# A graph-attention edge stage: counting every 16th key, a weight-stationary second expert layer, eight row buffers

## The reference

```
x = relu(sum over 32 paths of bn-conv(1x1, 3x3, 1x1)(x) + x)      # convolution
t = t + local attention(layernorm(t))                              # 7x7 window, 8 heads
t = t + mixture of experts(layernorm(t))                           # gates from a graph attention
```

```
h = x_flat @ W_gat                      # [M, 4 heads, 4 experts]
e = leaky_relu(a_src[src] + a_dst[dst]) # one value per edge and head
alpha = softmax of e over the edges of one dst
agg = segment_sum(h[src] * alpha, dst)  # then layernorm, mean over heads: scores
w = softmax of the two best scores
out += g[e] * (gelu(x @ W1[e] + b1[e]) @ W2[e] + b2[e])   # for 4 experts, 64 -> 128 -> 64
```

## Time and profile before

| | us |
|---|---|
| runs, median of 3 (lowest, highest) | 5598.91 (5587.48, 5601.15) |
| profiled execution, first to last instruction | 6624.5 |
| of it TensorE busy | 3002.6 (45%) |
| VectorE busy | 3002.1 (45%) |
| GpSimd busy | 2970.5 (45%) |
| ScalarE busy | 1456.9 (22%) |

### The profile page before, as it was taken

How to read it: one execution, slowest core, us unless ns; L and a number is a source line. 1 busy time by engine, 2 the same in 40 slices (tenths; PEclk the granted TensorE clock), 3 DMA queues, 4 the chain that set the end, 5 groups by cost and what they waited for, 6 DMA issues and landing times. The chain is left out here.

```text
span 6624.5 us, 60648 instructions
## 1 busy us (share of the span) xinstructions
PE 3002.6 (45%) x16592; PEld 2109.7 (32%) x16592; DVE 3002.1 (45%) x4301; ACT 1456.9 (22%) x5679; POOL 2970.5 (45%) x3274
## 2 busy tenths in 40 slices
PE   2888888869999760000444241311313130130620
PEld 1445455458888650000233120200202120120410
DVE  5888888649999731010899120110101011010358
ACT  0334343348888510000000010000000000010110
POOL 1000000026667537777000657575675757667045
PEclk9788888769999855555555555555555555555555
DMA  6566556646666450000000011110111111011143
GB/s 141 87 95 96 94 94 95 95 75 102 101 104 103 87 146 8 8 7 8 3 3 3 10 37 25 34 28 14 45 15 34 25 34 28 14 45 15 58 166 118
DMA packets 583690, 381.06 MB, mean 58 GB/s; under 512 B 404996, under 2 KB 524852, under 8 KB 577748
## 3 DMA queue, kind: packets, MB, share of 16 engines
q1 hardware_dynamic: 384376, 216.58, 14.6%
q10 hardware_dynamic: 89403, 109.89, 9.4%
q0 software_dynamic: 109728, 52.69, 6.7%
HBM read 232.80 MB, written 145.29 MB: 57 GB/s over the span
## 5 line engine op out<-in xcount | busy, mean ns | idle before, releaser
L1569 POOL DMA_INDIRECT e_row<-scratch_table,e_edge x2048 | 2014.2, 983 | 989.2 <-issue 680.8
L1750 PE MATMUL f_psY<-f_w,f_hid 128*128 128x64 f32 x1568 | 363.0, 425 | 1657.4 <-ACT f_hid L1701 1292.2
L1633 DVE TENSOR_TENSOR f_y<-f_psY,f_b 128x1024 f32<-128x1024 f32 x49 | 59.8, 1219 | 2298.5 <-DMA scratch_t<-t 1711.2
L1750 PEld LDWEIGHTS f_psY<-f_w,f_hid 128*128 128x128 f32 x1568 | 342.5, 330 | 1753.4 <-ACT f_hid L1701 1371.8
L1608 DVE TENSOR_TENSOR i_hot<-f_psH,i_digit 128x1024 bf16<-128x1024 f32 x512 | 582.3, 1211 | 640.0 <-DMA scratch_parts<-h2p 356.8
L1701 ACT ACTIVATE f_hid<-f_psH,f_b 128x512 f32<-128x512 f32 x196 | 131.4, 687 | 2933.9 <-PE f_psH L1745 1351.7
L1733 PE MATMUL f_psH<-i_hot 128*128 128x128 bf16 x2048 | 264.8, 310 | 958.3 <-DVE i_hot L1608 761.2
L964 POOL MEMSET a_wproj<- 128x128 f32 x1 | 0.2, 210 | 1367.4 <-POOLq L161 1367.4
L1077 ACT ACTIVATE prob<-psS,low 128x100 f32<-128x100 f32 x1568 | 514.1, 373 | 61.9 <-DVE low L1110 61.9
L1733 PEld LDWEIGHTS f_psH<-i_hot 128*128 128x128 bf16 x2048 | 197.3, 140 | 1025.7 <-DVE i_hot L1608 825.7
L472 PE MATMUL psH<-h,c_w 128*128 128x448 f32 x1008 | 511.5, 595 | 3.8 <-ACT h L584 2.0
(11 more groups left out here) (281 smaller groups left out, 5329.9 us busy)
## 6 DMA issues: line engine op xcount, KB each, us to landing
stack<-scratch_parts ACTq DMA_DIRECT2D x504, 112.0 KB
e_row<-scratch_table,e_edge POOLq DMA_INDIRECT x2048
scratch_y<-f_y ACTq DMA_DIRECT2D x49, 512.0 KB
scratch_state<-e_state SPq DMA_DIRECT2D x16, 1536.0 KB, 6.0
g_y<-scratch_y SPq DMA_DIRECT2D x24, 1024.0 KB
val<-scratch_vpad SPq DMA_DIRECT2D x672, 35.0 KB
scratch_parts<-h2p ACTq DMA_DIRECT2D x56, 336.0 KB, 3.3
keys<-scratch_kpad SPq DMA_DIRECT2D x112, 155.0 KB
```

The costliest lines, as they stand in the source:

```text
L1569: pool.indirect_dma_start(out=row[s][:, f, :], out_offset=None, in_=table_dram, in_offset=bass.IndirectOffsetOnAxis(ap=edge[s][:, 0, f:f + ...
L1750: m = pe.matmul(psY[par][:, j, e * C:(e + 1) * C], hid[e][:, j * 128:(j + 1) * 128], w2[:, e, :], start=True, stop=True)
```

## The change

It changes five things together.

First, the count. `Index` stores digits only for the last key of each group of 16 (`digit` is [128, 2, 128], `GROUP` = 16). The one-hots and matmuls count these: 16 groups instead of 256. The running sum gives, for each node, the one group of 16 keys in which its run ends (`group_ix`, semaphore `grouped`).

Second, GpSimd gathers these groups, 128 indirect DMAs of 64-byte rows of the sorted keys, one per column of nodes; VectorE counts how many of the 16 keys are at most the node's number, and so has the exact end of each run; its begin is the end of the node before, for a row's first node fetched from the partition above with a small DMA. Then the positions are `placed` as before.

Third, GpSimd's order: key groups, row gathers of chunk 0, first node's a_dst and the 128 scatters, row gathers of chunks 1 to 15. The small store after the scatters goes to SP.

Fourth, `AHEAD` = 8 row and edge buffers. To have the room, the one-hot tiles lie in the last row buffer, the zeros in `e0` and the keys in `part`. All loops of the phase are written out, with constant waits.

Fifth, the experts' second layer holds the weights still: `w2` is padded so that two experts share one 128-channel output, 4 matmuls of 512 columns a tile; the result has channels on partitions (`scratch_y` is [256, tokens]). ScalarE adds the bias while it copies from PSUM. Where ScalarE's exponentials of the chunks stand among the tiles is a list, `EXPS_AFTER`. `finish_phase` loads y by channel and turns it on TensorE, 16 transposes a chunk, into PSUM, from where VectorE scales it; TensorE's first turn stands before the transposes of the carries.

```diff
-AHEAD = 4
+AHEAD = 8
+KEYS_BEFORE, RUNS_BEFORE = 0, 1
+EXPS_AFTER = (14, 15, 16, 17, 18, 22, 25, 29, 33, 36, 40, 44, 47, 49, 49, 49)
...
+        group = part_i[:, 0:EF // GROUP]
+        lasts = dst[:].rearrange("p (g k) -> p g k", k=GROUP)[:, :, GROUP - 1]
...
-                for s in range(AHEAD):
-                    gather(0, s)
-                pool.wait_ge(const_in, 48)
-                pool.indirect_dma_start(out=b_first[:], out_offset=None, in_=adst_dram,
...
+                def group_keys():
+                    pool.wait_ge(grouped, 1)
+                    for t in range(128):
+                        pool.indirect_dma_start(out=keys[:, t, :], out_offset=None, in_=key_rows,
+                                                in_offset=bass.IndirectOffsetOnAxis(ap=group_ix[:, t:t + 1], axis=0)).then_inc(keys_in, 16)
...
+                for c in range(NFC):
+                    if c == KEYS_BEFORE:
+                        group_keys()
+                    if c == RUNS_BEFORE:
+                        first_of_run()
+                    gather(c)
...
-                with dve.Fori(0, NFC // 2) as turn:
-                    for par in range(2):
-                        dve.wait_ge(digit_in[par], (turn + 1) * 16)
-                        for g in range(GROUPS):
+                for g in range(GROUPS):
+                    dve.wait_ge(hot_used, g)
...
+                done(dve.tensor_scalar(inc[:], inc[:], float(GROUPS_ALL - 1), None, ALU.min))
+                dve.tensor_copy(group_ix[:], inc[:]).then_inc(grouped, 1)
...
+                dve.wait_ge(keys_in, 16 * 128)
+                done(dve.tensor_scalar(keys, keys, SRC_BITS, NODES - 1, ALU.logical_shift_right, ALU.bitwise_and))
+                done(dve.tensor_copy(keyf, keys))
+                dve.wait_ge(const_in, 48)
+                done(dve.tensor_tensor(keyf, keyf, node_id[:].unsqueeze(2).to_broadcast([128, 128, GROUP]), ALU.is_le))
+                done(dve.tensor_reduce(inside[:], keyf, AX.X, ALU.add))
+                dve.scalar_tensor_tensor(upto[:], inc[:], float(GROUP), inside[:], ALU.mult, ALU.add).then_inc(summed_up, 1)
...
+                for c in range(NFC):
+                    sp.wait_ge(scanned, c + 2)
+                    sp.dma_start(state_view[c], state[c % 2][:]).then_inc(state_out[c % 2], 16)
+                    if c + AHEAD < NFC:
+                        sp.dma_start(edge[c % AHEAD][:], edge_dram[c + AHEAD]).then_inc(edge_in[c % AHEAD], 16)
...
-                        for j in range(ZT // 128):
-                            m = pe.matmul(psY[par][:, j, e * C:(e + 1) * C], hid[e][:, j * 128:(j + 1) * 128], w2[:, e, :],
-                                          start=True, stop=True)
+                        m = pe.matmul(psY[par][:, e // 2, :], w2[:, e, :], hid[e][:], start=e % 2 == 0, stop=e % 2 == 1)
...
+                def turn(k):
+                    s, (lo, hi) = k % SLOTS, CHUNKS_AT[k]
+                    pe.wait_ge(y_in[s], loads(k))
+                    wait(pe, scale_done, k - 1)
+                    for j in range(hi - lo):
+                        for a in range(2):
+                            m = pe.transpose(psM[k % 2][:, j, 2 * a:2 * a + 2, :].rearrange("p e c -> p (e c)"),
+                                             y[s][:, a, j * 128:(j + 1) * 128], ident[:])
+                    m.then_inc(y_turned, 1)
```

More of the change, by code:

```diff
@@ L1227, in step @@
             dve.wait_ge(self.done, 5)
-            dve.tensor_copy(out[:, :, 5, :], chunks(part_i)).then_inc(self.digits, 1)
+            dve.tensor_copy(self.digit[:, 1, :], group).then_inc(self.digits, 1)
         elif i == 7:
@@ L1464, in edge_phase @@
         b_first = sb("e_b_first", [128, GHEADS])
[L1465 to L1468, removed]
+        iota = sb("i_iota", [128, 128]); before = sb("i_before", [128, 128]); node_id = sb("i_node_id", [128, 128])
+        digit = sb("i_digit", [128, 2, FC])
         zero = sb("i_zero", [128, 128], BF16)
@@ L1480, in edge_phase @@
         part = sb("e_part", [128, FC, GH])
-        w1 = sb("f_w1", [C, EXPERTS, 128]); b1 = sb("f_b1", [128, EXPERTS]); w2 = sb("f_w2", [128, EXPERTS, C])
-        b2 = sb("f_b2", [128, EXPERTS * C])
+        zeros = e0
+        keys = part[:].bitcast(I32)
+        keyf = state[0][:, :, 0:GROUP]
+        spare = row[AHEAD - 1][:].rearrange("p f c -> p (f c)").bitcast(BF16)
+        hot = [[spare[:, (2 * i + d) * HOT * 128:(2 * i + d + 1) * HOT * 128].rearrange("p (c x) -> p c x", x=128) for d in range(2)] for i in range(2)]
@@ L1527, in _ @@
                 for c in range(NFC):
[L1528 to L1532, removed]
+                    sp.dma_start(flat[c], zeros[:].rearrange("p f h -> p (f h)")).then_inc(b_zeroed, 16)
@@ L1587, in _ @@
-                with pool.Fori(1, NFC // AHEAD) as turn:
-                    for s in range(AHEAD):
-                        gather(turn, s)
+                def group_keys():
[3 more added lines that the diff above has]
+                                                in_offset=bass.IndirectOffsetOnAxis(ap=group_ix[:, t:t + 1], axis=0)).then_inc(keys_in, 16)
@@ L1711, in both @@
-                def both(turn, last):
-                    for par in range(2):
-                        for q in range(par * PER, (par + 1) * PER):
-                            gelus(turn, q, not last or q < 2 * PER - 1)
-                        exps(turn, par)
-                with act.Fori(0, NFC // 2 - 1) as turn:
-                    both(turn, False)
-                both(NFC // 2 - 1, True)
-                gelus(NFC // 2, 0, False)
-                act.wait_ge(y_out[0], 16 * (TILES_Z // 2 + 1))
@@ L1724, in _ @@
+                for par in range(2):
+                    act.wait_ge(y_out[par], 16 * ((TILES_Z + 1 - par) // 2))
             @block.tensor
@@ L1814, in finish_phase @@
         of_slot = lambda k: range(k % SLOTS, k + 1, SLOTS)
-        loads = lambda k: 16 * sum(1 + spans_of(*CHUNKS_AT[i]) for i in of_slot(k))
+        loads = lambda k: 16 * len(of_slot(k))
         stores = lambda k: 16 * sum(spans_of(*CHUNKS_AT[i]) for i in of_slot(k))
@@ L2049, in _ @@
                 m.then_inc(turned, 1)
+                turn(0)
                 pe.wait_ge(carried, 1)
@@ L2053, in _ @@
                 m.then_inc(turned_back, 1)
+                pe.wait_ge(fix_limited, 1)
+                for k in range(1, NCH):
+                    turn(k)
             @block.scalar
@@ L2130, in build_program @@
         table_phase(nc, io, range(N), t2, z, table, adst, index=index)
-    edge_phase(nc, io, z, table, adst, digit, edge, node, first, b, state, y)
-    finish_phase(nc, io, state, node, first, ends, table, adst, y, t2, out)
+    with ExitStack() as lasting:
+        edge_phase(nc, lasting, io, ordered, z, table, adst, digit, edge, node, first, b, state, y)
+        finish_phase(nc, lasting, io, state, node, first, ends, table, adst, y, t2, out)
 def kernel(**inputs):
```

287 lines of the change are left out of this document (147 added, 140 removed).

## The result

The changed kernel takes 5777.45 us (median of 4 runs, 5769.58 to 5781.56) against 5600.03 us before: ratio 1.0312, 95% interval 1.0294 to 1.0329, slower by 177 us. The forecast was 5756 us, from 5590 to 5850.

The account below looks back on a forecast made before the run. GpSimd's chain of gathers was taken to set the end of the edge stage. The terms summed to +157.4 us on 5661, giving 5819; less the 62 us offset, 5756 us, range 5590 to 5850.

Parts of the forecast that it names:

- the 1025 us: Profiled span 6624.5 us against 5598.9 timed; read as recording delaying TensorE's completions, absent from timed runs; removing delays gives 5661.
- start wait: Before the first gather: GpSimd waits for the short count, first gather at 2494.8 instead of 2448.2, +46.6 us (44 to 60).
- tables: Table stage: the smaller digit store holds SP's next issue for less time, -5 us (0 to -11).
- key gathers: Edge stage: 128 more indirect DMAs on GpSimd at 1.304 us each, +166.9 us (160 to 179).
- chunk 0's wait: After the scatters: with eight row buffers GpSimd no longer waits for chunk 0's scan, -40.1 us.
- 2048 row gathers: Edge stage: the first 512, at 1.352 us, might go at 1.304; between -24 and nothing, -12 us taken.
- tail: After the last gathers: the last chunk's b scan is now ahead of its rows, -2 us.
- finish: Last phase: chunk 0's turn on TensorE stands ahead of the carry transposes and sums gathers wait, +3 us (0 to +10).
- offset of -62 us: The timed 5599 lies 62 us below the 5661 left after removing delays from the trace; carried over to the forecast.
- third rival: Slower still: 1.352 us spacing is what gathers beside an undisturbed TensorE cost, for all of them; 5854 us, chance 6%.
- Waits real: First rival: TensorE's completions come late in timed runs too, so GpSimd's idle time is real; faster, 4918 us, chance 13%.
- the second: Second rival: a share of the wait is real, the count ending some 150 us after 512 gathers; 5600 us, chance 5%.

Follow-up runs that it names:

- before_again: The kernel before, unchanged, profiled and timed once more: ratio 0.9997 to the kernel before, profiled span 5618.5 us.
- late_keys: The changed kernel with key groups gathered after chunk 0's rows and scatters after chunk 1's: 5733.57 us, ratio 1.0224 to the kernel before.
- full_count_eight: The changed kernel with the count of all keys put back, no key groups, scatters behind chunk 3: 5568.86 us, ratio 0.9926 to the kernel before.
- one_key_gather: The changed kernel with one of the 128 key gathers instead of all: 5620.41 us, ratio 1.0006 to the kernel before.
- before_eight_buffers: The kernel before with eight row and edge buffers, scatters still behind chunks 0 to 3: 5587.66 us, ratio 0.9956 to the kernel before.
- before_short_count: The kernel before counting only every 16th key, without key groups: 5605.15 us against 5610.79, ratio 0.9993.
- weights_in_psum: full_count_eight with the edge weights written to PSUM and one output buffer for the experts: 5533.30 us, ratio 0.9833 to the kernel before.

## Why the prediction was right, point by point

Direction and size hold, and so does the mechanism of the change: GpSimd's chain of indirect DMAs sets the end, the full count was hidden, the key groups and the start wait are new on the chain. The cause that the prediction gave for the 1025 us was wrong, and the sum came out closer than its terms. The terms, from the start of one step to the start of the next in the profiles of before_again (5618.5 us) and of the kernel after (5774.2):

| step | predicted, us | in the profiles, us | timed alone |
|---|---|---|---|
| start wait | +46.6 | +43.0 (2446.12 in late_keys to 2489.11) | 49 (late_keys) |
| tables | -5 | -4.6 (full_count_eight 2450.67, late_keys 2446.12; same chip) | |
| key gathers | +166.9 | +162.7 | 171 (one_key_gather) |
| chunk 0's wait | -40.1 | -31.9 (33.2 between last scatter and next gather; 1.3) | -25 (before_eight_buffers) |
| 2048 row gathers | -12 | +0.7 (2655.6; 2656.3) | |
| tail | -2 | -1.2 (28.3; 27.1) | |
| finish | +3 | -9.2 (279.4; 270.2) | |
| sum | +157.4 | +155.7 by the spans | +177 |

(The rows add up to 159.5. Of the 3.8 us between, 3.6 come from the first gather: it starts at 2454.24 us in before_again and at 2450.67 in full_count_eight, on another chip.)

**Luck in the sum.** The forecast was 12.7 us too low for the row gathers and 8.2 too low for chunk 0's wait, and 12.2 too high for the finish, 4.2 for the key gathers and 3.6 for the start. They cancel to 2 us. That the sum fits so well is luck; that the two large terms fit within 5 us is not.

**Start, keys, tables.** Right within 5 us each. (A third of the 11.20 us of the earlier trace rows would be 3.7 for the tables, not the 5 that was taken.) The spacing of the key gathers was 1.272 us, between the 1.25 and the 1.304 of the prediction, since no scan stands beside them.

**The reading of the 1025 us.** Right that the timed kernel does not have them, by the sum, and this carried the sign of the forecast. Wrong in its cause: "the cost of recording". Two consequences of that cause, stated in the prediction, failed. In the changed kernel late completions were to let TensorE do only three or four tiles in 167 us; the 248 matmul records in the 163 us of key gathers are 15 tiles and a half. And recording would have to hit every profile, while before_again shows none of it. The sign that the prediction had set for this reading (a span near 5820 us and a timed run within 1.5% of it) came true all the same: it fits any cause that is missing from timed runs, and could not tell recording from one disturbed execution. That a wrong cause led to the right conclusion rests on the sum alone, which took the delays out whatever they were. Why TensorE's completions came late in that execution stays open.

**The offset of -62 us.** It was carried as if it lay in the scale of the trace. It did not: before_again spans 5618.5 us where the sum gave 5661, and 39.8 of these 42.5 us are the first stretch (692.1 us for 512 gathers; 652.3 from 2454.24 to 3106.54 here), 8.2 chunk 0's wait (41.4 against 33.2, from the last scatter's start to the next gather's), less 6.0 by which the stage starts later. So the high spacing of that stretch, 1.352, was the disturbance as well: in it GpSimd idled for 0.86 us every 22.4 us, once for each pair of one-hot tiles, and 27 of the 512 gathers took over 1.1 us; in before_again there is neither. This decides the third rival: 2048 row gathers take the same in both kernels, and 1.352 never returns. The 12 us taken off for it was a step to leave out.

**Chunk 0's wait.** Mis-sized: 33.2 us undisturbed, of which 30.2 show as a wait, so that 31.9 go where the forecast took 40.1 from the disturbed trace. The timed saving of the buffers alone, 25 us (0.28 to 0.60%), agrees with that within its interval.

**The finish.** Wrong in sign. The turn before the carries costs what was said (carries are turned at 5522.38, 2.6 us after they were ready), but the sums gathers, which bound this phase, get shorter by 164.0 - 143.5 = 20.5 us, because the scaling pass no longer holds them. Only 9.2 us of it reach the end: 2.2 us go to the later start of these gathers, and behind the last of them the phase takes 61.5 us where it took 52.3. Part of that is VectorE's, which now waits longer for its chunks (21.8 us in total before its scaling passes in full_count_eight, 14.3 in before_eight_buffers); the rest no run attributes. The prediction weighed what the transposes cost TensorE and not what VectorE's operand in PSUM does to GpSimd.

**What is left.** The profiles give +155.7, the timed medians +177. The kernel before has a median of 5619.6 us where before_again was profiled, and of 5600.0 beside the changed kernel. With these 19.6 us added, the spans give 175.3. How they lie among the steps no run shows, so a row of the table can be off by several us: in before_short_count and before_eight_buffers, on another chip than before_again, the 2048 row gathers take 2646.6 and 2650.3 us where it has 2655.6.

**The rivals.** Waits real, in full or in part: out by before_short_count (0.9993). The condition of the second was worked out wrongly: a one-hot pair at 2.9 us would end the count some 55 us after the 512 gathers (2452.4 + 256 x 2.9 = 3195 against 3140), and 150 us take some 3.3; measured beside gathers is 2.26. Slower still: out by the spacing of 1.298.

## What to carry to other kernels

Before a trace is used as a price list, put its span beside the timed runs; where they differ, find which intervals make up the difference and price each step by intervals that the sum clears, and read a second execution before naming a cause. Where GpSimd's indirect DMAs are the chain that ends last, shrinking VectorE's and TensorE's work buys nothing (before_short_count), and any step put ahead of the first gather, or answered by more gathers, is paid in full: put it beside gathers that are issued anyway. Then look at what VectorE reads while they are issued: an operand moved to PSUM was worth more here (39.9 us in the traces) than eight buffers (29.9).

## What the runs showed of the hardware

- A VectorE pass with two SBUF inputs holds an indirect DMA that GpSimd starts beside it until the pass is over: 2.94 or 3.37 us for one of 0.94 to 1.00. Over the 128 sums gathers of before_again, the 29 mostly beside the scaling pass took 1.84 us on average, the 34 beside nothing 1.00. With one input in PSUM the same pass, no slower itself (2.29 us), holds hardly any: 1.02 us on average for 34 in the kernel after. Beside the products of weights_in_psum it is 0.94 to 0.95 us for 45.
- One indirect DMA of 128 rows costs 1.25 us from start to start (the median) whether its rows have 64 or 80 bytes. With a pause of about 3.2 us after every 163 to 167 us of them the mean is 1.27, and 1.31 for scatters of 16-byte rows.
- One profiled execution was 18% longer than the program's time, with the same 60648 instructions, at the same granted clock, and with TensorE's completions reaching VectorE some 20 us late beside gathers.
